# Attention and mixture-of-experts block: shared experts' matmuls dealt out between attention's steps

## The reference

```
xn  = layernorm(x)                        # x: 2 batches x 1024 tokens x 512
out = x + attention(xn) + ffn(xn)

attention: 16 heads of 32; S = Q K^T / sqrt(32), causal; softmax(S) V; then @ Wo.T
ffn:   scores = sigmoid(xn @ router.T); top 2 groups of 4, then top 2 of 8 experts
       out  = sum over the 2 chosen experts of weight * mlp(xn)      # 8 experts, width 352
            + mlp_shared(xn)                                         # width 704 = 2 x 352
mlp(x) = (silu(x @ gate.T) * (x @ up.T)) @ down.T
```

## Time and profile before

| | |
|---|---|
| time, median of 3 runs (lowest, highest) | 1208.49 us (1207.11, 1211.96) |
| span of the profiled execution, first to last instruction | 1173.5 us |
| median time less that span | 35.0 us |
| PE busy in the span | 1083.7 us (92%) |
| DVE, ACT, POOL busy | 766.0, 604.8, 529.5 us |
| DMA over the span | 132 MB, 112 GB/s |

### The profile page before, as it was taken

The page is one execution under the profiler, slowest core; times in us unless marked ns, Lnnn a source line. Parts: engine busy times, 40 slices in busy tenths (PEclk is TensorE's granted clock), DMA queues, the critical chain, the costliest instruction groups (busy, mean ns, idle before and its releaser), DMA issues. The chain is left out here.

```text
span 1173.5 us, 22057 instructions
## 1 busy us (share of the span) xinstructions
PE 1083.7 (92%) x5635; PEld 796.9 (68%) x5636; DVE 766.0 (65%) x1508; ACT 604.8 (52%) x1223; POOL 529.5 (45%) x565
## 2 busy tenths in 40 slices
PE   5979998999999599899999998997979999999994
PEld 4838887777777366565566655655867777777773
DVE  6822322422222679998898988975567888777882
ACT  4532222111111089798797988992145555555551
POOL 0008306470000079798897988993003333333331
PEclk9999999999999589999999999998999999999998
DMA  5953558500010834454544445406813333333332
GB/s 207 313 200 130 202 223 290 2 1 2 36 37 36 207 91 109 121 120 115 129 103 119 119 117 126 118 2 208 278 70 71 73 73 63 67 69 72 72 73 36
DMA packets 92290, 131.98 MB, mean 112 GB/s; under 512 B 47696, under 2 KB 56208, under 8 KB 90032
## 3 DMA queue, kind: packets, MB, share of 16 engines
q1 hardware_dynamic: 81776, 110.32, 32.5%
q0 software_dynamic: 9856, 20.53, 9.5%
q10 hardware_dynamic: 576, 0.26, 0.1%
HBM read 82.37 MB, written 48.70 MB: 112 GB/s over the span
## 5 line engine op out<-in xcount | busy, mean ns | idle before, releaser
L839 POOL TENSOR_TENSOR prob_lo<-prob,prob_hi 128x128 fp32r<-128x128 f32 (+2 forms) x320 | 331.1, 1068 | 77.8 <-ACT prob_hi L885 42.8
L915 DVE TENSOR_REDUCE maxima<-ps_m 128x1 f32<-128x512 f32 (+3 forms) x384 | 198.1, 546 | 23.8 <-PE ps_m L984 15.2
L875 ACT ACTIVATE prob<-ps_s 128x512 f32<-128x512 f32 (+3 forms) x384 | 182.6, 486 | 29.4 <-POOL prob_lo L839 19.4
L885 ACT ACTIVATE prob_hi<-prob 128x128 fp32r<-128x128 f32 (+2 forms) x320 | 167.7, 524 | 25.3 <-PE ps_o L1033 19.9
L980 PE MATMUL ps_m<-ks,qs 96*128 96x512 f32 (+3 forms) x384 | 161.7, 429 | 10.6 <-DMA ks<-qk_hi 9.6
L1535 POOL DMA_INDIRECT out<-work,rows x39 | 61.9, 1587 | 235.0 <-DVE rows L1581 111.7
L1620 DVE TENSOR_TENSOR rw_lo<-gu_sb,rw_hi 128x704 fp32r<-128x704 f32 x156 | 138.8, 893 | 41.2 <-ACT rw_hi L1555 35.6
L1008 PE MATMUL ps_s<-qs,ks 97*128 97x512 f32 (+3 forms) x384 | 140.6, 366 | 17.8 <-ACT prob L875 14.4
L1555 ACT ACTIVATE rw_hi<-gu_sb 128x704 fp32r x156 | 123.3, 793 | 40.0 <-PE ps_ru L1653 30.9
L1031 PE MATMUL ps_o<-prob_hi,vs 128*66 128x512 f32 (+3 forms) x384 | 138.6, 361 | 1.5 <-POOL prob_lo L839 1.5
L1033 PE MATMUL ps_o<-prob_lo,vs 128*66 128x512 f32 (+3 forms) x384 | 130.0, 339 | 0.0
(11 more groups left out here) (215 smaller groups left out, 2449.4 us busy)
## 6 DMA issues: line engine op xcount, KB each, us to landing
v_rows<-work SPq DMA_DIRECT2D x16, 512.0 KB, 2.9
qk_hi<-work SPq DMA_DIRECT2D x8, 1024.0 KB, 3.9
qk_lo<-work SPq DMA_DIRECT2D x8, 1024.0 KB, 6.5
qs<-qk_hi SPq DMA_DIRECT2D x64, 128.0 KB, 2.6
ks<-qk_hi SPq DMA_DIRECT2D x64, 128.0 KB, 3.0
vs<-v_rows SPq DMA_DIRECT2D x32, 256.0 KB, 3.6
gu_sb<-in_gate SPq DMA_DIRECT2D x32, 176.0 KB, 3.4
gu_sb<-in_up SPq DMA_DIRECT2D x32, 176.0 KB, 3.4
```

The costliest lines, as they stand in the source:

```text
L839: nc.gpsimd.tensor_tensor(prob_lo[:, c % NP, 0:w], prob[:, c % NP, 0:w], prob_hi[:, c % NP, 0:w].bitcast(F32), ALU.subtract).then_inc(lo_p ...
L875: nc.scalar.activation(prob[:, c % NP, 0:w], ps_s[c % NS][:, 0:w], ACT.Exp, scale=SCALE).then_inc(exp_done, 1)
L885: nc.scalar.activation(prob_hi[:, c % NP, 0:w], prob[:, c % NP, 0:w], ACT.Copy).then_inc(hi_act, 1)
L915: nc.vector.reduce_max(maxima[:, slot, at:at + 1], scores, AX.X).then_inc(m_read, 1)
```

## The change

`shared_phase` is gone. `attend_phase` now also holds its work, and is written out in full (no loop), 426 steps long (`ALL`):

- **Fill.** `fill_counts` deals the 864 matmuls out over steps 12 to 407 so that an estimated cost of each step is level; in the body of the attention that is 24 per head, 1 to 4 per step. They stand between `score` and `turn_o`/`value`. They share two banks, `ps_f`. Silu is made from tanh on ACT and two DVE operations with three operands (`gated`, `hid`). A unit is one half of the shared experts on one token block; there are 8.
- **Buffers.** `ps_m` goes from 3 banks to 2, `ps_o` from 2 to 1 (a half's first `value` waits for the copy of the half before), `prob` from 6 to 4 places, with 6 for `prob_hi` and 5 for `prob_lo`. `hi` is on ACT for all 12 steps; `lo` on POOL for 10 and on DVE for 2, other steps than before.
- **Transposes.** xt no longer stays in SBUF through the shared experts' work: `project_phase` stores it to HBM by block (8 stores of 1 MB, `xt_blocks`), and waits for them; each unit loads its block (2 MB) in attention.
- **Weights.** The second half's shared weights are loaded and split in pieces in mid-attention. The routed experts' gate, up and down weights are no longer loaded in attention and one piece per tile, but expert by expert: three in `out_phase` (at tiles 1, 6 and 11), the others in `routed_phase`, each when the third before it has landed; ACT and PE wait there for `experts_ready`.
- **Slots.** POOL does 48 of the placing steps ahead of its first `lo`, the rest one per step between them, then the 32 indirect DMAs, one per step.

```diff
+    xt_dram = nc.dram_tensor("xt_blocks", [NTB, P, 2, KC, TBW], F32, kind="Internal").ap()
...
 def project_phase
+                def store_xt(t):
+                    cols = slice(t * TBW, (t + 1) * TBW)
+                    for n, xt in enumerate((xt_hi, xt_lo)):
+                        sp.dma_start(xt_dram[t, :, n], xt[:, :, cols].bitcast(F32)
+                                     ).then_inc(xt_stored, 16)
...
-                pipeline(sp, CH, U, [(0, load), (0, load_shared), (2, store)])
+                pipeline(sp, CH, U, [(0, load), (0, load_shared), (2, store), (4, store_blocks)],
+                         back=1)
+                sp.wait_ge(xt_stored, 32 * NTB)
...
 def attend_phase
-    AHEAD = 2 * NB
-    EXP, HI, LO, VALUE = AHEAD + 1, AHEAD + 2, AHEAD + 4, AHEAD + 8
+    EXP, HI, LO, VALUE = AHEAD + 1, AHEAD + 2, AHEAD + 3, AHEAD + 7
+    FILL = fill_counts([step_cost(s) for s in range(ALL)], UNITS * PER_UNIT, 12, STEPS + AHEAD, 228.0)
...
+        NP, NPH, NPL = 4, 6, 5
+        NM = 2
...
+                def load_xt(unit):
+                    wait(sp, up_done, NF * unit)
+                    sp.wait_ge(xt_stored, 32 * NTB)
+                    sp.dma_start(xt[:, :, :, :].bitcast(F32), xt_dram[unit % NTB]
+                                 ).then_inc(xt_loaded, 16)
...
+                        if unit and g == ACC_AT[unit]:
+                            store_acc(unit - 1)
+                        if g == ACC_AT[unit]:
+                            load_base(unit)
+                    if 0 < g <= HEADS:
+                        load_values(g - 1)
+                    for k in range(NF):
+                        if g == RAW_AT[k]:
+                            load_gate_up(k)
+                        if g == DOWN_RAW_AT[k]:
+                            load_shared_down(k)
...
+                    for t in range(NT):
+                        for k in range(2):
+                            nc.gpsimd.indirect_dma_start(
+                                slots_dram, bass.IndirectOffsetOnAxis(slot_of[:, t, k:k + 1], 0),
+                                entry[:, t, k, :], None).then_inc(entries_stored, 16)
+                            yield
...
+                def lo(s):
+                    n = s % NB
+                    if n in LO_POOL:
+                        first, w = span(n)
+                        wait(pool, hi_ready, s + 1)
+                        wait(pool, pv_done, s - NPL + 1)
+                        nc.gpsimd.tensor_tensor(prob_lo[:, s % NPL, 0:w], prob[:, s % NP, 0:w],
+                                                prob_hi[:, s % NPH, 0:w].bitcast(F32),
+                                                ALU.subtract).then_inc(lo_pool, 1)
+                    next(placing_steps, None)
+                for _ in range(48):
+                    next(placing_steps, None)
+                steps([(LO, lo)])
...
+                    for k in DOWN_SPLIT_AT.get(s, ()):
+                        f0, w = FCH[k]
+                        act.wait_ge(y_done, 4 * (LAST + 1))
+                        act.wait_ge(d_raw_loaded, 16 * (k + 1))
...
+                for s in range(ALL):
+                    for lag, stage in ((0, maximum), (AHEAD, score)):
+                        if 0 <= s - lag < STEPS:
+                            stage(s - lag)
+                    shared(s)
+                    for lag, stage in ((TURN, turn_o), (VALUE, value), (ROW, turn_row)):
+                        if 0 <= s - lag < STEPS:
+                            stage(s - lag)
...
 def out_phase
-                pipeline(sp, NT, U, [(0, load), (0, load_down), (2, store)])
+                pipeline(sp, NT, U, [(0, load), (0, first_experts), (2, store)], back=NT)
...
 def routed_phase
+                for e in range(E):
+                    sp.wait_ge(expert_loaded[e % len(FIRST_AT)], 64 * (e // len(FIRST_AT) + 1))
+                    sp.sem_inc(experts_ready, 1)
+                    if e + len(FIRST_AT) < E:
+                        load_expert(sp, e + len(FIRST_AT), gate, up, down, gu_sb, d_sb,
+                                    expert_loaded)
```

More of the change, by code:

```diff
@@ new lines, in maximum @@
+                def maximum(s):
+                    g, c = s // NB, s // NB % HS
+                    t, k0, w = PIECES[s % NB]
+                    if s % NB == 0:
+                        pe.wait_ge(head_loaded[c], 96 * (g // HS + 1))
+                    wait(pe, m_read, s - NM + 1)
+                    diagonal = k0 + w == P * (t + 1)
+                    last = nc.tensor.matmul(ps_m[s % NM][:, 0:w], qs[0:ROWS, c, t * P:(t + 1) * P],
+                                            ks[0:ROWS, c, k0:k0 + w], start=True, stop=not diagonal)
+                    if diagonal:
+                        last = nc.tensor.matmul(ps_m[s % NM][:, w - P:w], late[:, :], eye[:, :],
+                                                start=False, stop=True)
+                    last.then_inc(m_done, 1)
@@ L999, in score @@
[L999 to L1013 removed]
+                        last = nc.tensor.matmul(ps_s[s % NS][:, 0:P], eye[:, :], late[:, :],
@@ L1060, in out_phase @@
+def out_phase(nc, wo, gate, up, down, ident, attended, gu_sb, d_sb, out, y_tile, y_stored,
+              slot_table, rows, rows_ready, xn_dram, gathered, passed, expert_loaded):
     with ExitStack() as ctx:
```

1123 lines of the change are left out of this document (617 added, 506 removed).

## The result

On one chip, four runs each, the changed kernel took 1246.4 us in the median (1243.7 to 1248.1) and the kernel before 1208.9 (1207.1 to 1212.0): a ratio of 1.0317, 95% interval 1.0288 to 1.0347. The forecast was 1224.5, slower by 16; it is slower by 37.5. The direction is as forecast and the time lies inside the range, but the loss is more than twice the one forecast.

What follows compares the result with a forecast made beforehand. PE was taken to bound attention. First fill at 223.8, 545 us of steps, 34 of waits, 8.1 and 3 at the end put the output phase 13 us later; with 3 behind it, span 1189.5, time 1224.5, range 1182 to 1254.

Steps and rivals of the forecast that it cites:

- first fill (step 12): Start of attention: PE starts at 215.7 us behind the Q and K stores; twelve maxima without fill, then step 12 at 223.8.
- steps 12 to 407 with their stalls: Attention with fills: 545 us of PE's own stream, 1.38 us a step, and 34 us of waits.
- last fill to the output phase: End of attention: 8.1 us from last score to last normalization, and 3 us more for POOL's load of the slot table.
- output and routed phases: Phases behind attention: 3 us longer together, 2 for loads in the output phase and 1 for gathers in the routed one.
- time less span: Whole kernel: the median time taken as 35.0 us above the profiled span, so span 1189.5 gives time 1224.5.
- the transitions: PE in attention: a 512-column matmul right behind a diagonal's costs 0.09 us more, sixteen a head; 23 us in all.
- handshakes: Rival, in attention: PE, ACT and POOL wait for each other, 0.45 us at 64 ends, 29 us; time 1253, chance 0.18.
- (e): PE in attention: with one `ps_o` bank a half's next value waits for the copy, 0.05 us x 64 = 3 us.
- PE runs closer to its bare pace: Rival, in attention: transitions and waits come to less than 35 us, not 57; time 1179, under 1202.5; chance 0.27.
- ACT's stop for `d_raw`: Near step 219: ACT waits 7 us and PE about 5 for a piece of the second half's down weights.
- POOL blocked by DVE: Rival, steps 34 to 65: DVE's work blocks POOL's slot DMA issues, 20 us more; time 1244, chance 0.08.
- the slot row: Profile row of POOL's slot DMAs, 0.96 us each; by it POOL's 32 transfers cost 18 us in steps 34 to 65.

Runs made afterwards that it cites:

- e6_xt: Changed kernel with the eight xt blocks stored one per projection chunk, ahead of that chunk's own stores: 1230.3 us, 1.0185 of the kernel before.
- e1_row: Changed kernel with PE's turn of a head's normalized row issued one step later: 1232.7 us, 1.0378 of the kernel before.
- e2_order: Changed kernel with each step's fills between the maximum and the score matmuls: 1229.8 us, 1.0349 of the kernel before.
- e13_last: Changed kernel with each step's fills behind the AV matmuls and the row's turn: 1219.7 us, 1.0285 of the kernel before.
- e15_lastbest: Changed kernel with row's turn later, slot transfers spread, raw loads ahead, token blocks and slot table early, fills last in each step: 1154.4 us, 0.9731 of the kernel before.
- e10_table: Changed kernel with POOL loading the slot table at step 240 instead of behind its last `lo`: 1240.5 us, 1.0453 of the kernel before.
- e8_after: Changed kernel, unchanged, run again beside its variants on another chip: 1248.8 us, 1.0518 of the kernel before there.
- e12_best: As e15_lastbest, but with the fills between maximum and score: 1169.9 us, 0.9874 of the kernel before.

## Why the prediction came out as it did

The reckoning against the changed kernel's trace, in us from the start:

| term | forecast | measured | miss |
|---|---|---|---|
| first fill (step 12) | 223.8 | 219.4 | -4.4 |
| steps 12 to 407 with their stalls | 579 | 624.7 | +45.7 |
| last fill to the output phase | 11.1 | 15.5 | +4.4 |
| output and routed phases | 375.5 | 382.4 | +6.9 |
| time less span | 35.0 | 4.4 | -30.6 |

The sum is +22, the distance from 1224.5 to 1246.4.

**Start.** The first `ps_m` was forecast for 215.7 and came at 205.8, outside the 210 to 220 named. The mechanism was right, as e6_xt shows. The pair of stores ahead of xt went out at 166.43 instead of 169.67, and from it to SP's first load of attention (200.17) the 12.6 MB took 33.7 us, where 39.4 stood in the sum. The rate of 323 GB/s was taken from a lone pair's 6.5 us; the queue moved 373. That the time of a lone pair holds something that a queue pays only once is argued, not shown.

**Steps 12 to 407: the step that failed.** The prediction took a head's time as PE's own stream and nothing else: "So PE is the bound", with 10.9 us a head and the fills' 201 us, 16.5 us a head. It was 17.85. Times 33 heads that is the 45 us. The price of the transitions, the term I called least certain, was right: 0.08 us each where 0.09 stood. What was missing are waits of PE inside the head, which the sum had at nothing: the turn of the row behind DVE's normalization (0.5 us, e1_row), and the score that comes too soon for ACT's exponential (0.4 us, with cheaper neighbours 0.5 to 0.7, e2_order and e13_last). With both moved, the same instructions run at a commonest pitch of 16.4 to 16.6 us, near the 16.5 of the sum; over the last ten heads it is 16.6 to 16.9. I had checked that DVE and ACT have room in the mean, and not how late their one result that PE waits for is.

The rival "handshakes" was right about one of the two. It said that ACT, held at `o_copy` until PE's value ends, gives the next exponential late. The changed kernel's ACT, and then PE's next score:

```profile
711.96 0.60 ACT L1203 ACTIVATE o_copy<-ps_o 66x512 f32<-66x512 f32 x1 [2.00 <-PE ps_o L1424]
...
713.46 0.59 ACT L1187 ACTIVATE prob<-ps_s 128x512 f32<-128x512 f32 x1
```

```profile
714.09 0.51 PE L1399 MATMUL ps_s<-qs,ks 97*128 97x512 f32 x1 [0.60 <-ACT prob L1187]
```

ACT stands for 2.00 us, then copies, and comes to the exponential behind a `hi` and a tanh of the fills. From 592 to 791 us PE waits twelve times for over 0.1 us at a score, and each time 1.65 to 2.13 us behind the start of an `o_copy` for which ACT had stood 1.4 to 2.1 us, with no gap on ACT since. Together that is 2.8 us in eleven heads, 0.25 a head where the rival had 0.9. The other 0.5 us, the turn of the row, it did not have. Its size came near the loss only because of that second wait. PE is never seen to wait for the copy of `ps_o` itself, the 3 us of (e). "PE runs closer to its bare pace" is refuted for this kernel, and e15_lastbest is that rival, with six edits more.

**Stalls.** 34 us forecast; the heads over 17.9 us hold about 40, and 33 heads of 17.85 us leave 36 of the 624.7. Among the slot transfers the three heads hold 18.7 us where 18 were forecast for them, but that agreement is luck: POOL's transfers do come two microseconds apart (2.46), yet spreading them gives back 10.5 us, and most of the rest is PE's 4.8 us of idling behind ACT's wait for the row of maxima, which the sum did not have. ACT's stop for `d_raw` is 9.8 us instead of 7, PE's 8.2 instead of 5; waits for xt are small. POOL blocked by DVE is refuted: the slot transfers take 990 ns in the median, 962 before. So of the two prices weighed in the prediction, the one from the slot row was right. That rule of the Trainium skill ("SBUF — State Buffer", "Who interferes with whom") gave 1244, close to the time measured, and is not the reason of it.

**End and the phases behind.** The table cost 6.3 us, not 3 (e10_table). The output phase took 3.6 us more and the routed 6.3, of which one tile's wait of 3.5 us for its rows behind the expert loads; 3 together were forecast. In e8_after the output phase took 60.8 us instead of 63.6, so part of this is one execution against another.

**The base.** I set the forecast against an execution of 1173.5 us and added the 35 us to the median as if they lay outside the program. All but 1.8 lie in it, and depend on the chip and the execution. This error hid 30 of the 53 us by which the span was missed (1189.5 forecast, 1242.0 measured): that the time still lies inside the range is luck, not reckoning. On a chip like that of e8_after the change costs 61 us.

## What to carry over

When work is dealt out into an engine's gaps, price the waits of that engine one by one: for each instruction that takes another engine's result, the time from that result's cause to its need, at the new pace. An average load of 65% on the others says nothing about them. Look one engine further too: the result that PE waited for in nearly every head was late because DVE had stood behind an instruction of POOL. The dealing-out itself was sound: with the fills last in each step, the turn one step later, the slot transfers spread, the loads that something waits for first in their queue, and the table read early, the kernel is 2.7% faster than the one before (0.9731, 0.9688 to 0.9774).

## What the runs showed of the hardware

- DVE's normalization of 128x128, both inputs in SBUF, took 0.29 us where POOL was idle (852.20 in the changed kernel) and 0.95 us in the mean over 64. By the Trainium skill, page "SBUF — State Buffer", section "Who interferes with whom", a VectorE instruction with two SBUF inputs contends with a GpSimd one that reads SBUF. The traces agree, and give the size: it ends 0.15 us behind the end of the `lo` that was under way when it started, in 59 of 59 cases in the changed kernel, 63 of 63 in e12_best, and 56 of 63 in the kernel before. What differs is how much of the `lo` is left at its start, 0.83 us in the mean in the changed kernel and 0.24 in the kernel before, whose mean of 0.42 is the shorter for it.
- A matmul of 512 columns directly behind a mask's (bf16, 128 columns) holds PE for 0.315 us with 128 columns of weights, 0.29 with 96, and 0.264 with 66 (the AV matmul); 0.231 otherwise. The change of type isn't what makes it: behind the turn of the row, f32 in the records and 128 columns wide, it is 0.314 too with 128 columns of weights, and behind an AV matmul of 128 columns 0.283 and 0.258 with 128 and 96 columns of weights, while behind one of 256 columns or more it is 0.23. So the price goes with how short the matmul ahead is and how many columns of weights come next.
- The same kernel before took 1185 to 1188 us on four chips and 1205 to 1209 on two occasions, while the changed kernel, measured on two chips, moved by 2.
